# Causal attention in a decoder kernel: scores of four heads on four 32-row groups of TensorE, one exponential for four heads, norms from squares added on VectorE

## The reference, cut to what matters

```python
def _L1_attn_ref(x, Wqkv, bqkv, Wout, bout):
    B, S, E = x.shape
    H = HEADS                      # 16
    D = E // H                     # 32
    scale = E ** (-0.25)
    qkv = jnp.einsum('bse,fe->bsf', x, Wqkv) + bqkv
    q, k, v = jnp.split(qkv, 3, axis=-1)
    sin, cos = _rope_sincos(S, E, x.dtype)
    q = _rotate(q, sin, cos)
    k = _rotate(k, sin, cos)
    q = _l2_normalize(q) * scale   # over all 512 features
    k = _l2_normalize(k) * scale
    ...
    scores = jnp.einsum('bhqd,bhkd->bhqk', q, k)
    causal = jnp.tril(jnp.ones((S, S), dtype=bool))
    scores = jnp.where(causal, scores, mask_value)
    attn_w = jax.nn.softmax(scores, axis=-1)
    attn = jnp.einsum('bhqk,bhkd->bqhd', attn_w, v)
    return jnp.einsum('bse,fe->bsf', attn, Wout) + bout
```

## Time and profile before

| | us |
|---|---|
| median of 3 runs | 2788.03 |
| lowest and highest run | 2782.67, 2789.25 |
| the profiled execution, its own time | 2787.26 |
| span of its trace | 2785.5 |
| causal stage, first projection to the last output rows | 1485.54 to 1916.13 |

### The profile page before, as it was taken

The page is one execution under the profiler, slowest core; times in us unless marked ns, Lnnn a source line. Parts: engine busy times, 40 slices in busy tenths (PEclk is TensorE's granted clock), DMA queues, the critical chain, the costliest instruction groups (busy, mean ns, idle before and its releaser), DMA issues. The chain is left out here.

```text
span 2785.5 us, 34483 instructions
## 1 busy us (share of the span) xinstructions
PE 2124.0 (76%) x12315; PEld 1350.6 (48%) x12315; DVE 1838.7 (66%) x2425; ACT 1340.7 (48%) x2235; POOL 1012.5 (36%) x651
## 2 busy tenths in 40 slices
PE   2787666045698888988856999998896677689996
PEld 0455553012566666666634777775443233244442
DVE  4359883966677777777723554554353697899975
ACT  0013223552676677666632322323454685556655
POOL 1014532305246777777623333334110000443430
PEclk7998777576899999999968999999998898899998
DMA  3225555004448999999760000002132540000001
GB/s 137 60 97 193 192 196 201 0 0 137 166 154 245 260 255 249 255 261 257 181 234 0 1 1 0 0 0 106 46 113 83 204 152 1 0 1 1 1 1 61
DMA packets 123676, 313.50 MB, mean 113 GB/s; under 512 B 29569, under 2 KB 49537, under 8 KB 119810
## 3 DMA queue, kind: packets, MB, share of 16 engines
q1 hardware_dynamic: 102466, 260.69, 26.5%
q0 software_dynamic: 21056, 50.84, 9.2%
HBM read 219.59 MB, written 92.68 MB: 112 GB/s over the span
## 5 line engine op out<-in xcount | busy, mean ns | idle before, releaser
L1407 DVE SCALAR_TENSOR_TENSOR x_part<-x_group,x_scale,x_part 128x256 f32<-128x256 f32 x660 | 288.0, 477 | 144.7 <-ACT x_part L1349 136.9
L1296 PE MATMUL x_group<-x_xt,x_gu 128*128 128x256 f16 x2640 | 347.1, 275 | 1.8 <-DVE x_xt L1399 0.9
L1349 ACT ACTIVATE x_part<-x_group,x_scale 128x256 f32<-128x256 f32 x660 | 276.2, 471 | 123.1 <-PE x_group L1296 117.2
L1262 POOL TENSOR_TENSOR x_part<-x_part 128x512 f32<-128x512 f32 x165 | 235.3, 1430 | 197.2 <-DVE x_part L1407 197.2
L1296 PEld LDWEIGHTS x_group<-x_xt,x_gu 128*128 128x128 fp8e4 x2640 | 237.6, 98 | 85.7 <-issue 31.7
L1633 POOL TENSOR_TENSOR c_pt<-c_pt,const_tables 128x256 f32<-128x256 f32 x128 | 127.8, 1019 | 280.6 <-ACT c_pt L1741 280.3
L1313 PE MATMUL x_y_ps<-x_d_hi,x_h_hi 128*128 128x512 f32 x330 | 160.2, 485 | 68.8 <-DVE x_h_lo L1420 66.8
L2420 POOL TENSOR_TENSOR f_part<-f_part 128x1024 f32<-128x1024 f32 x44 | 120.4, 2735 | 187.9 <-DVE f_part L2447 187.9
L155 PE MATMUL mean_n<-residual,const_tables 128*128 128x512 f32 x160 | 80.0, 652 | 137.4 <-PEq L734 103.5
L2318 PE MATMUL f_group<-f_x_hi,f_raw 128*128 128x512 f16 x352 | 138.9, 395 | 32.3 <-DVE f_part L2447 24.9
L1253 POOL DMA_INDIRECT mixed_rows<-x_y,moe_rows x94 | 150.1, 1597 | 31.1 <-issue 20.8
(11 more groups left out here) (335 smaller groups left out, 5290.9 us busy)
## 6 DMA issues: line engine op xcount, KB each, us to landing
x_d_hi<-down_hi SPq DMA_DIRECT2D x50, 768.0 KB, 5.6
x_d_lo<-down_lo SPq DMA_DIRECT2D x50, 768.0 KB, 5.9
x_gu<-codes_gu SPq DMA_DIRECT2D x50, 384.0 KB, 5.8
p_w<-d_s SPq DMA_DIRECT2D x17, 768.0 KB, 7.5
down_hi<-p_hi SPq DMA_DIRECT2D x17, 768.0 KB, 3.9
down_lo<-p_lo SPq DMA_DIRECT2D x17, 768.0 KB, 6.2
aux<-ct SPq DMA_DIRECT2D x2, 4096.0 KB, 17.0
cross_values<-y_v_out SPq DMA_DIRECT2D x16, 512.0 KB, 3.0
```

Of the source, the lines that this page charges most:

```text
L1262: pool.tensor_tensor(x[:, 0, :, :], x[:, 0, :, :], x[:, 1, :, :], ALU.add).then_inc(summed, 1)
L1296: mm = pe.matmul(group_ps[s % 2][:, q, :], codes[:, q, col:col + P], xt[u][:, k, q, :], start=k == 0, stop=k == 1)
L1349: act.activation(part[n % PARTS][:, q, o % 2, :], group_ps[s % 2][:, q, :], ACT.Copy, scale=scale[v][:, o, q:q + 1]).then_inc(ev_act, 1)
L1407: dve.scalar_tensor_tensor(x, group_ps[s % 2][:, 2 + q, :], scale[v][:, o, 2 + q:3 + q], x, ALU.mult, ALU.add).then_inc(ev_dve, 1)
```

## The change

All within the causal stage; the core of the diff follows.

- **Scores.** The spread keys are gone. Each of the four heads of a chunk uses its own 32 rows of `k_sb` and `q_sb`, and writes to its own bank of `s_ps` (four banks, a single buffer). The scale goes into the exponential.
- **Exponential and mask.** One ScalarE instruction for four heads (128 x 1536), one GpSimd instruction for their diagonal blocks (128 x 1024), in three buffers.
- **Norms.** VectorE squares as before, then adds the four chunks of squares (two additions), and one matmul of 512 columns sums over the partitions, after the values in place of before them.
- **Buffers.** `out_ps` and `den_ps` hold two chunks and not four, keys are double buffered, `xb` and its GpSimd copy are gone, the semaphores are one pair per task, and all batches are written out with no loop.
- **Order.** TensorE's order within a batch is written out: score group, queries, last value group of the batch before, score group, keys, value group, score group, values, value group, norms, score group, output, value group. VectorE's: square, divide, square, add, value rows, divide, normalise, output rows.

```diff
-        kp = [sb(f"kp{i}", [P, 4, S]) for i in range(2)]
...
-        pt = [sb(f"pt{i}", [P, 3, P]) for i in range(RING)]
-        at = [sb(f"at{i}", [P, C, S]) for i in range(2)]
-        out_ps, den_ps, work = ps("out_ps", [P, C, S]), ps("den_ps", [P, C, S]), ps("work", [P, C, S])
+        q_sb, k_sb = two("q", [P, C, S]), two("k", [P, C, S])
+        v_sb = two("v", [P, 2, D])
+        pt = [sb(f"pt{i}", [P, 4, 3, P]) for i in range(PT_RING)]
+        at = two("at", [P, C, S])
+        s_ps = ps("s", [P, 4, 4, P])
+        out_ps, den_ps = ps("out_ps", [P, 2, S]), ps("den_ps", [P, 2, S])
+        work = ps("work", [P, C, S])
...
+            def queries(b):
+                if b >= 1:
+                    pe.wait_ge(rooted, b)
+                if b >= 3:
+                    pe.wait_ge(o_read, b - 2)
...
+            def norms(b):
+                pe.wait_ge(v_read, b + 1)
+                pe.wait_ge(summed, b + 1)
+                pe.matmul(work[:, 2:4, :], g.const("ones"), sums[:, :, :], start=True, stop=True).then_inc(norm_done, 1)
...
+            def score(b, c):
+                n = GROUPS * b + c
+                if c == 0:
+                    pe.wait_ge(qk_ready, 2 * b + 2)
+                if n >= 1:
+                    pe.wait_ge(exped, n)
+                for k in range(2):
+                    for j in range(4):
+                        r = slice(32 * j, 32 * j + 32)
+                        out = s_ps[:, j, 0:2, :] if k == 0 else s_ps[:, j, 2, :]
+                        mm = pe.matmul(out, k_sb[b % 2][r, c, k * P:(k + 1) * P], q_sb[b % 2][r, c, k * P:S],
+                                       start=True, stop=True)
+                mm.then_inc(s_done, 1)
...
+            for b in range(-1, B):
+                now, following = b >= 0, b + 1 < B
+                if now:
+                    score(b, 0)
+                if following:
+                    queries(b + 1)
+                if b >= 1:
+                    values(b - 1, 3)
+                if now:
+                    score(b, 1)
+                if following:
+                    keys(b + 1)
+                if now:
+                    values(b, 0)
+                    score(b, 2)
+                if following:
+                    value_rows(b + 1)
+                if now:
+                    values(b, 1)
+                if following:
+                    norms(b + 1)
+                if now:
+                    score(b, 3)
+                if b >= 1:
+                    output(b - 1)
+                if now:
+                    values(b, 2)
+            values(B - 1, 3)
+            output(B - 1)
...
+            def exponential(b, c):
+                n = GROUPS * b + c
+                act.wait_ge(s_done, n + 1)
+                if n >= PT_RING:
+                    act.wait_ge(av_done, n - PT_RING + 1)
+                act.activation(pt[n % PT_RING][:, :, :, :], s_ps[:, :, 0:3, :], ACT.Exp, scale=D ** -0.5).then_inc(exped, 1)
...
+            keep = g.const("causal").unsqueeze(1).unsqueeze(1).to_broadcast([P, 4, 2, P])
+            for n in range(GROUPS * B):
+                pool.wait_ge(exped, n + 1)
+                diagonal = pt[n % PT_RING][:, :, 0:3:2, :]
+                pool.tensor_tensor(diagonal, diagonal, keep, ALU.mult).then_inc(masked, 1)
...
+            def add_squares(b):
+                step(dve.tensor_tensor(pairs[:, :, :, :], squares[:, :, 0:2, :], squares[:, :, 2:4, :], ALU.add))
+                dve.tensor_tensor(sums[:, :, :], pairs[:, :, 0, :], pairs[:, :, 1, :], ALU.add).then_inc(summed, 1)
...
+            def normalise(b):
+                dve.wait_ge(rooted, b + 1)
+                if b >= 2:
+                    dve.wait_ge(s_done, GROUPS * (b - 1))
+                step(dve.tensor_scalar(nrm[:, :, :], nrm[:, :, :], 1e-12, None, ALU.max))
+                step(dve.reciprocal(nrm[:, :, :], nrm[:, :, :]))
+                for k, (y, x) in enumerate(((q_sb, q_raw), (k_sb, k_raw))):
+                    dve.tensor_tensor(y[b % 2][:, :, :], x[:, :, :], bc(nrm[:, k, :], 1, [P, C, S]), ALU.mult)\
+                       .then_inc(qk_ready, 1)
...
+            for b in range(-1, B):
+                now, following = b >= 0, b + 1 < B
+                if following:
+                    step(square(b + 1, 0))
+                if b >= 1:
+                    divide(b - 1, 1)
+                if following:
+                    step(square(b + 1, 1))
+                    add_squares(b + 1)
+                    value_rows(b + 1)
+                if now:
+                    divide(b, 0)
+                if following:
+                    normalise(b + 1)
+                if b >= 1:
+                    output(b - 1)
```

More of the change, by code:

```diff
@@ L1510, in _ @@
                    .then_inc(out, 1)
-LAG = 2
-RING = 8
 X_RING = 16
@@ L1561, in causal_attention @@
 def causal_attention(nc, g, a):
[L1564 to L1572, removed]
+    GROUPS, PT_RING = H1 // 4, 3
     with ExitStack() as ctx:
@@ L1613, in sides, with batch @@
[L1613 to L1639, removed]
+        def batch(b):
+            return slice(b * S, (b + 1) * S)
@@ L1641, in _ @@
         @block.tensor
         def _(pe):
-            def project(w, x):
-                for m in range(C):
-                    for c in range(C):
[L1646 to L1686, removed]
+            def project(wx, x, m):
+                for c in range(C):
+                    mm = pe.matmul(work[:, m, :], wx[:, c, m * P:(m + 1) * P], x[:, c, :], start=c == 0, stop=c == C - 1)
+                return mm
@@ L1696, in values @@
                             else:
-                                mm = pe.matmul(y[r, c, P:S], wt, x[:, 2, :], start=False, stop=True,
+                                mm = pe.matmul(y[32 * j:32 * j + 32, o, P:S], wt, x[:, j, 2, :], start=False, stop=True,
                                                skip_group_check=True)
-                mm.then_inc(av_done, 4)
[L1701 to L1704, removed]
-                    for name, of, n in sides(h, b, last, following):
-                        side(name, of, 1 - i, n)
-                    if h >= LAG and (h - LAG) % 4 == 3:
-                        values(b, i, (h - LAG) // 4, last)
@@ L1710, in _ @@
-            pe.wait_ge(folded, 1)
-            for name in FRONT:
-                if name == "keys":
-                    pe.wait_ge(folded, 2)
-                if name == "values":
-                    pe.wait_ge(v_loaded, 32)
-                side(name, 0, 0, use(0, name), name == "queries")
-            side("nothing", -1, 0, len(FRONT))
-            pe.wait_ge(o_loaded, 32)
-            every_batch(pe, heads)
-            side("output", B - 1, 1, LAST_USES + 1)
+                mm.then_inc(av_done, 1)
@@ L1749, in _, with copy, root @@
-            every_batch(act, heads)
+            def copy(b, done, x, bias_x, read):
+                act.wait_ge(done, b + 1)
+                if b >= 1:
+                    act.wait_ge(qk_ready, 2 * b)
+                for m in range(C):
+                    last = act.activation(x[:, m, :], work[:, m, :], ACT.Identity, bias=bias_x[:, m:m + 1])
+                last.then_inc(read, 1)
+            def root(b):
+                act.wait_ge(norm_done, b + 1)
+                act.activation(nrm[:, :, :], work[:, 2:4, :], ACT.Sqrt).then_inc(rooted, 1)
@@ new lines, in divide, with output @@
+            def divide(b, o):
+                pair = slice(2 * o, 2 * o + 2)
+                dve.wait_ge(av_done, GROUPS * b + 2 * o + 2)
+                if b >= 2:
+                    dve.wait_ge(o_done, b - 1)
+                step(dve.reciprocal(at[b % 2][:, pair, :], den_ps[:, :, :]))
+                dve.tensor_tensor(at[b % 2][:, pair, :], out_ps[:, :, :], at[b % 2][:, pair, :], ALU.mult)\
+                   .then_inc(divided, 1)
+            def output(b):
+                dve.wait_ge(o_done, b + 1)
+                for m in range(C):
+                    x = g.xt[:, m, batch(b)]
+                    last = dve.scalar_tensor_tensor(x, work[:, m, :], bias["bo"][:, m:m + 1], x, ALU.add, ALU.add)
+                last.then_inc(o_read, 1)
@@ L1830 @@
+            divide(B - 1, 1)
+            output(B - 1)
 CROSS_KINDS = ("k", "v", "q")
```

180 lines of the change are left out of this document (72 added, 108 removed).

## The result

The changed kernel takes 2710.04 us (median of 3 runs, 2709.0 to 2711.14) against 2788.03: a ratio of 0.9726, 95% interval 0.9709 to 0.9743. The forecast was 2709. Its profiled execution took 2711.14 us with a span of 2709.3, 76.2 less than before. All of that is in the causal stage: its last output rows start at 1839.81 and not at 1916.13, 76.3 earlier. The stage itself gained a little more: its first projection started at 1487.14 in this execution and at 1485.54 in the one before, so it lasts 352.7 where it lasted 430.6, 77.9 less.

The account below looks back on a forecast made before the run. TensorE was taken to bound the causal stage. 1524.4 + 39.9 + 39.0 + 5 × 39.8 + 34.7 = 1837.0 for the last output rows, 79 us less, hence 2709 us; range 2697 to 2722 (0.64), high end 2740 including rival 1.

Parts of the forecast that it names:

- Row groups: Causal scores: four heads on separate 32-row groups run side by side, 0.85 us a group, 3.4 a batch instead of 11.3.
- rival 1: Score groups: weight loads run one after another, 1.9 us a group, 2733 us in all; chance 0.14.
- Rival 2: Score groups: the row groups don't overlap, 2.8 us a group, 2759 us in all; chance 0.07.
- Norms: TensorE's norms slot: sixteen passes become two of 512 columns, 1.1 us for 3.46; VectorE additions 1.2 + 0.7, hidden.
- ScalarE and GpSimd: Per score group: exponential 1.5 us, mask 2.7 to 4.1; exponential not a bound, masks with over 15 us until needed.
- What is late next: Between batches: VectorE's divide, normalise, output rows delay next scores and queries, 1.2 us a batch; batches 2 to 6 take 39.8.
- The clock: TensorE's clock after idle: 1.7 us each added before batch 0's scores, in batch 0 and in the tail.
- front: Stage start to first score: 1485.5 to 1522.7, with 1.7 us added for idle TensorE, so 1524.4.
- tail: From the last batch's first score to the last output rows: 34.7 us, where before it took 40.13.
- batches 0 and 1: First two batches of the causal stage: 39.9 us, where before it took 44.45, then 39.0.
- rival 3: VectorE's chain lengthened by meeting GpSimd's mask: 2 us in each of seven batches, 2723 us; chance 0.10.
- rival 4: Slower than before: idle drops TensorE's clock; loss needs about 30% of its work at half speed; example 2835; chance 0.04.

Follow-up runs that it names:

- experiment 1: Changed kernel with score matmuls contracting over all 128 rows instead of each head's own 32; 2756.4 us, ratio 0.989.
- Experiment 3: Changed kernel without the two VectorE additions, norms by 16 matmul passes again, in the new place behind the values; 2721.24 us, ratio 0.9763.
- experiment 4: Kernel before the change, with only squares added on VectorE and one 512-column norms matmul, in the old order; 2788.64 us, ratio 1.0.
- experiment 5: Changed kernel with exponential and mask of a group split into four instructions each, head by head; 2709.93 us, ratio 0.9714.
- Experiment 10: Changed kernel with ScalarE copying out the output product and its bias, VectorE adding it to the residual later, except last batch; 2706.42 us, ratio 0.9712.
- Experiment 9: Changed kernel with unread matmuls filling TensorE's idle time before the first scores of batches 0 and 1; 2706.06 us, ratio 0.9714.
- yardstick: The changed kernel itself, unaltered, run again in the second set of experiments; 2709.0 us, ratio 0.9716.
- experiment 6: Changed kernel with one unread 1024-element VectorE spread per batch, between dividing the first half and normalising; 2742.84 us, ratio 0.9835.
- experiment 2: Changed kernel with the two loops of a score group exchanged, each head's 256- and 128-column products adjacent; 2710.33 us, ratio 0.9722.
- experiments 8: Changed kernel with an added VectorE spread per batch in the chain, plus three unread matmuls before the scores of batches 2 to 7; 2733.95 us, ratio 0.9806.
- 11: Changed kernel with ScalarE output copy, unread matmuls around batch 0, and front norms ahead of value products with three unread matmuls; 2697.16 us, ratio 0.9686.

## Why the prediction was right

*Row groups.* Forecast 0.85 a group for "side by side", measured 0.87. The 16 loads of a group, which rival 1 would have in a row at 1.74 us, fit in 0.74 in the changed kernel's timeline of weight loads, and each is as long as one over 128 rows (median 185 ns in the changed kernel against 191), so it is the overlap that saves and not a shorter load:

```profile
1685.67 0.74 PEld L1654 LDWEIGHTS c_s<-c_q,c_k 32*128 32x128 f32 x16 [0.20 <-DVE c_k L1784]
```

Rival 2's mechanism was made in experiment 1: 2.72 for its 2.8, and 2756 for its 2759.

*Norms.* 1.06 for 1.1. The two additions were to take 1.2 and 0.7; the second takes 2.72 in a middle batch, as it collides with a mask, but it lies under the value products as forecast. Experiment 3 gives its value in this order, 1.9 a batch; experiment 4 shows that the same edit was worth nothing in the old one.

*ScalarE and GpSimd.* The exponential takes 1.45 (1.5 forecast), the mask 2.36 in the seam above (2.7 to 4.1 forecast, from rows of other instructions, too high). Neither is waited for in a middle batch; experiment 5 shows it.

*What is late next.* VectorE's chain, as forecast, but with its size off: 0.72 a batch for 1.2, since the keys were ready at V + 10.34 and not V + 10.75, and the queries started at V + 12.05 and not V + 12.45. That makes 39.34 for 39.8, 2.3 us over five batches. Experiment 10 removes this wait and only this: 38.64, the forecast's 38.6 for TensorE's own work.

*The clock* was the mis-sized term, and it was also put in the wrong places. The forecast charged 1.7 before batch 0 and 1.7 in it, both for the one idle stretch before batch 0's scores, and nothing for the idle stretch before batch 1's. In these rows of the changed kernel (timeline of TensorE) the front holds no such cost, and the work behind each of the stretches of 6.9, 4.5, 3.2 and 4.2 us runs slowly:

```profile
1487.14 10.08 PE L1603 MATMUL c_work<-residual,c_wq 128*128 128x256 f32 x32 [17.27 <-PEq L130]
...
1524.28 1.66 PE L1654 MATMUL c_s<-c_q,c_k 32*128 32x256 f32 x16 [6.93 <-DVE c_k L1784]
1525.87 9.51 PE L1603 MATMUL c_work<-residual,c_wq 128*128 128x256 f32 x32
...
1565.34 1.67 PE L1654 MATMUL c_s<-c_q,c_k 32*128 32x256 f32 x16 [4.51 <-DVE c_k L1784]
1566.93 9.46 PE L1603 MATMUL c_work<-residual,c_wq 128*128 128x256 f32 x32
...
1810.35 0.97 PE L1669 MATMUL c_out_ps<-c_pt,c_v 128*32 128x256 f32 x8 [3.22 <-DVE c_at L1793]
...
1830.91 8.86 PE L1603 MATMUL c_work<-c_at,c_wo 128*128 128x256 f32 x32 [4.21 <-DVE c_at L1793]
```

The front, first projection to first score, took 1524.28 - 1487.14 = 37.1. The forecast had 1522.7 - 1485.5 = 37.2 for it before it added the 1.7. Behind the idle stretch, the granted clock was 0.71 from 1524.3 to 1535.3, and score group and queries took 11.0 where they take 8.0 at full clock; batch 1 lost 3.0 in the same way. Experiment 9 fills both stretches and gets both back. In the tail two falls of the clock made a value group, a score group and an output projection longer by 1.2, 0.5 and 1.7, where one 1.7 was charged.

Counted from the start of the stage, the forecast's errors are these: front 1.8 too long, batches 0 and 1 3.8 too short (82.7 for 78.9), the five middle batches 2.3 too long, the tail 1.4 too short (36.1 for 34.7). Errors of both signs leave 1.2. The stage also started 1.6 later than in the execution before, which the change does not explain: in the yardstick's execution of the same kernel it started at 1484.0. Together 2.8: the last output rows came at 1839.8 and not 1837.0. The profiled execution was forecast at 2708 and came to 2711, and the median at 2709 and came to 2710. The mechanism was right term by term, but that the total comes within 1 us is in part luck.

*Rivals 3 and 4* did not come about in the middle batches of the changed kernel, by 0.46 us between clip and mask: experiment 6 puts 1.1 us before the clip and gets both, the collision (2.2 on top of the operation's 1.1) and the clock's fall (1.7), in every middle batch. The forecast's price for rival 3, 2 us a batch, was too low for what stands behind it. Even so that kernel stays 1.6% faster than the one before, so rival 4's condition for a loss is far off.

*What was not tested by itself.* Experiments 1 and 3 give back 46 and 11 to 12 of the 78 us. The other 20 or so lie, by the slots, above all in the mask's wait that went (2.4 a batch, with 0.7 come back elsewhere). No run has the new kernel with the old order or with the spreads, so whether the order or the missing spreads removed the mask's wait stays open.

## What to carry to other kernels

Work that uses few rows of the array gains from row groups even in fp32 and with a 128-column load for every product: look for padded operands first. When passes are taken off the engine that sets the pace, find the wait that follows them: the same cut of 2.4 us was worth 1.9 in the new order and nothing in the old one, where half of it became waits for VectorE and the clock fell more often. And measure the slack of a chain before leaving it: here 0.1 us at the scores and 0.46 at the clip separated a gain of 78 us from one of 45.

## What the runs showed of the hardware that was not expected

- Products on different row groups overlapped in both orders in which they were written, at 0.87 a group in the changed kernel and 0.88 in experiment 2 (1662.60 to 1663.48).
- A VectorE clip of 512 columns took 0.42 us alone and 2.58 beside a GpSimd mask; an addition of 512 columns 0.69 and 2.72 (changed kernel, front and middle batch). Reciprocals of the same size took 3.35 in both cases (at 1518.48 and 1679.80 of the changed kernel).
- The clock fell to its lower level behind idle stretches of 3.15 us in every middle batch of experiment 6, behind 2.4 us in every second batch of experiment 4 and once in six in the kernel before, and not behind the 0.7 us of the changed kernel. With the idle time filled by unread matmuls, it stayed at the upper one (1.00 in the windows of experiments 8, 9 and 11).
